# Attention stage: the 512-column products of TensorE that nobody reads are left out from the second batch on

## What is computed

```python
x = x + 0.5 * ffn(layernorm(x))          # 8 experts, top 2
x = x + attn(layernorm(x))
x = x + 0.5 * ffn(layernorm(x))

def attn(x):                              # B 8, S 256, E 128, H 16, HD 8
    q, k, v = (x @ w_q.T), (x @ w_k.T), (x @ w_v.T)      # as (B, S, H, HD)
    q, k = rope(q), rope(k)
    att = softmax(einsum('bqhd,bkhd->bhqk', q, k) / sqrt(HD))
    return einsum('bhqk,bkhd->bqhd', att, v).reshape(B, S, 128) @ w_o.T
```

## Time and profile before

| | us |
|---|---|
| median of 3 runs | 477.1 (476.74 to 477.88) |
| the profiled execution, its own time | 477.5 |
| its span, first to last instruction | 475.2 |
| TensorE busy | 400.3 |
| VectorE busy | 333.3 |
| ScalarE busy | 259.5 |
| GpSimd busy | 221.1 |

### The profile page before, as it was taken

How to read it: one execution, slowest core, us unless ns; L and a number is a source line. 1 busy time by engine, 2 the same in 40 slices (tenths; PEclk the granted TensorE clock), 3 DMA queues, 4 the chain that set the end, 5 groups by cost and what they waited for, 6 DMA issues and landing times.

```text
span 475.2 us, 10124 instructions
## 1 busy us (share of the span) xinstructions
PE 400.3 (84%) x3108; PEld 318.6 (67%) x3108; DVE 333.3 (70%) x1090; ACT 259.5 (55%) x525; POOL 221.1 (47%) x284
## 2 busy tenths in 40 slices
PE   4781885999899998989899999896889789999940
PEld 3551475989789875666766767673668679998830
DVE  4644762555877678778898988875537666558985
ACT  1332542766555646576675767573676256666610
POOL 4375653676553433133243542515035566645551
PEclk9786897999999997799999999999999799999975
DMA  9711531123211203992000000001111112133322
GB/s 269 285 53 37 173 117 50 40 63 86 65 51 41 74 24 117 331 320 59 2 23 13 12 14 13 24 8 35 35 39 47 51 50 62 57 109 95 107 63 70
DMA packets 33201, 37.78 MB, mean 80 GB/s; under 512 B 5504, under 2 KB 28032, under 8 KB 32752
## 3 DMA queue, kind: packets, MB, share of 16 engines
q1 hardware_dynamic: 28144, 27.36, 19.4%
q0 software_dynamic: 4544, 9.35, 5.9%
q10 hardware_dynamic: 464, 0.45, 0.5%
HBM read 26.71 MB, written 20.36 MB: 99 GB/s over the span
## 4 chain that ended last, share of the span: by engine, by line
PE 39%; DVE 10%; ACT 5%; issue 4%; another core or an unknown queue 2%; POOL 1%; POOLq 0%; DVEq 0%; ACTq 0%
PE ps L998 6%; PE ps L821 3%; PE ps L927 3%; PE ps L807 3%; PE ps L794 2%; PE ps L664 2%; DVE ring_lo L1882 2%; PE ps L882 2%; PE ps L822 2%; ACT stage L1356 2%; PE ps L1007 2%; PE ps L907 2%; PE ps L796 2%; PE ps L795 2%
## 5 line engine op out<-in xcount | busy, mean ns | idle before, releaser
L1882 DVE TENSOR_REDUCE ring_lo<-ps 128x4 fp32r<-128x1024 f32 x64 | 78.0, 1219 | 15.7 <-PE ps L916 15.6
L1300 ACT ACTIVATE stage<-ps 128x512 f32<-128x512 f32 x78 | 46.6, 597 | 76.9 <-PE ps L796 62.2
L1356 ACT ACTIVATE stage<-ps 128x1024 f32<-128x1024 f32 x64 | 65.4, 1022 | 21.2 <-PE ps L927 19.7
L821 PE MATMUL ps<-w_hl,ring_hi 128*128 x234 | 65.7, 349 | 7.4 <-issue 5.0
L1775 DVE TENSOR_TENSOR ring_hi<-ps,ring_hi 128x512 fp32r<-128x512 f32 x78 | 53.8, 690 | 16.4 <-ACT ring_hi L1307 12.0
L822 PE MATMUL ps<-w_hl,ring_hi 128*128 x312 | 61.4, 238 | 0.0
L537 POOL DMA_INDIRECT expert_y<-stage x39 | 38.3, 983 | 48.3 <-DVE stage L1783 45.4
L504 POOL DMA_INDIRECT sorted_x<-rows,place_at x32 | 31.9, 997 | 60.0 <-DVE place_at L1590 44.7
L537 POOL DMA_INDIRECT expert_y<-stage,arena x39 | 38.7, 993 | 40.7 <-DVE stage L1783 35.8
L1769 DVE TENSOR_TENSOR bx<-ps,bx 128x128 fp32r<-128x128 f32 x78 | 22.5, 289 | 50.1 <-ACT bx L1282 43.1
L822 PEld LDWEIGHTS ps<-w_hl,ring_hi 128*128 128x128 f32 x312 | 55.1, 195 | 0.0
(11 more groups left out here) (194 smaller groups left out, 963.2 us busy)
## 6 DMA issues: line engine op xcount, KB each, us to landing
sorted_x<-fill SPq DMA_DIRECT2D x8, 1096.5 KB, 16.7
stage<-w SPq DMA_DIRECT2D x16, 256.0 KB, 6.5
stage<-sorted_x SPq DMA_DIRECT2D x39, 64.5 KB
arena<-sorted_x SPq DMA_DIRECT2D x39, 64.5 KB
y_got<-expert_y SPq DMA_DIRECT2D x16, 128.0 KB, 2.3
stage<-expert_y SPq DMA_DIRECT2D x16, 128.0 KB, 2.4
x_tok<-x SPq DMA_DIRECT2D x4, 256.0 KB, 5.4
sorted_x<-rows,place_at POOLq DMA_INDIRECT x64
```

Of the source, the lines that this page charges most:

```text
L821: pe.matmul(both, bg_hi[:, s, c, :], w, start=(c == 0), stop=False, skip_group_check=True)
L1300: act.activation(g_full[:, s, :], ps[:, H_BANK, :], ACT.Gelu).then_inc(g_done, 1)
L1356: act.activation(prob[:, 2 * v:2 * v + 2, :], ps[:, at:at + 2, :], ACT.Exp, scale=SCALE)\
L1882: vec.tensor_reduce(shift_v[:, t, :, 24].rearrange("p (r g j) -> p r j g", r=2, g=2)[:, pair, 2 * jp:2 * jp + 2, :], ps[:, at:at + 2, :].r ...
```

## The change

All `keep_busy` products of the attention stage in batches 1 to 6 are left out, and the three at the start of batch 7: 21 + 12 + 6 + 10 = 49 products. With them go the waits that only they needed. Those of batch 0 stay, and so do the ten behind the start of batch 7. No other instruction is added, removed or moved, on any engine.

```diff
@@ step @@
-                if v == 0:
-                    pe.wait_ge(exp_done, STEPS * b + v + 1)
-                    keep_busy(EXP_BANK, 2 if b == 0 else 3)
+                if b == 0 and v == 0:
+                    pe.wait_ge(exp_done, 1)
+                    keep_busy(EXP_BANK, 2)
                 if scores_next:
                     scores_free(b + 1, v)
@@ batch, behind step 2 @@
                 if place_next:
                     if tail:
-                        scores_owned(b + 1, 3)
-                        keep_busy(2 * (3 % MAX_BUF), 2)
                         pe.wait_ge(y_ready, 2 * b - 1)
                     place(b + 1, q, 3, M1)
                 step(b, p, 3, place_next)
                 if place_next:
-                    if b:
-                        scores_owned(b + 1, 4)
-                        keep_busy(2 * (4 % MAX_BUF), 1)
-                    else:
+                    if b == 0:
                         pe.wait_ge(exp_done, STEPS * b + 4 + EXP_BUF)
                         keep_busy(EXP_BANK, 3)
                     pe.wait_ge(qk4_ready, 4 * b + 8)
@@ batch, behind step 4 @@
                     keep_busy(Y_BANK, 2)
                     router(FIRST_UNIT + b - 2)
                 elif b >= 2:
-                    scores_owned(b + 1, 5)
-                    keep_busy(2 * (5 % MAX_BUF), 2)
                     pe.wait_ge(yt_ready, b)
```

## The result

Medians of 20 executions each, on one chip: 473.47 us (468.76 to 479.75) against 475.87 us (474.26 to 480.58) of the kernel before. The ratio is 0.9953, interval 0.993 to 0.9976; ratios leave out the executions that took over 1.5% more than the fastest of the same kernel (here four of the 20, the profiled one among them), while medians and means are over all. The changed kernel is faster by 2.4 us, where the forecast was a time 2.8 us longer. The profiled execution took 477.69 us, and its span is 475.4 us; before it was 477.5 and 475.2. So the two profiles alone would show no difference, because this execution had the clock low for longer than most: the mean granted clock is 0.917 here and was 0.932 there.

What follows compares the result with a forecast made beforehand. The prediction took TensorE as the busiest engine, 400.3 of 475.2 us. From 477.5 us it took 3.4 for products on the path, added 6.2 for two clock falls (480.3), and forecast a median of 479.9 us, range 473.0 to 487.5.

Steps and rivals of the forecast that it cites:

- Start of the batch: Three products at the start of batches 1 to 7: 0 us in six batches, covered by ACT's copies; batch 7 taken as 0.
- The wait for "issue": PE's unexplained 2.03 us wait in batch 7, 5.5 us behind the scores, taken as what ends last there.
- Pair ahead of the fourth placing: Two products there in batches 1 to 6: 0.55 us gained in four batches, 0.48 in batches 4 and 5, 3.2 us.
- the single: One product ahead of the transposes in batches 1 to 6: 0 us, since the transposes wait for ACT's copy anyway.
- the router pair: Two products ahead of the router in batches 2 to 6: 0.3 us in batch 2, 0 later through DVE's queue.
- The price of low clock: From batch 0 against batch 1, steps 4 to 7: each us of low clock costs 0.32 us.
- The length of a fall and their sum: In the attention stage a fall lasts 6.5 to about 10 us and costs 3.1 us; two cost 6.2 us.
- The number of falls: Lean stretch from fourth placing to second projection, six batches: a fall in one batch in three, 2 falls; the weakest number.
- if a fall costs far from 3 us: Sign in the changed kernel's trace that the price from batch 0 doesn't carry over to the later batches.
- the clock holds everywhere: Rival: no fall in the attention stage, so the gain stands alone, 473.7 us or 472.8 with batch 7; chance 0.28.
- Falls in nearly every batch: Rival: 5 falls, at PE in steps 4 to 6 of each batch, 489.2 us; chance 0.10 for five or more.
- the gain is taken up: Rival: clock holds, but DVE or ACT's copies end last and the 0.55 us become PE idle time; 477.1 us, chance 0.07.

Runs made afterwards that it cites:

- e1: Only the three products at the start of batches 1 to 7 (21) left out of the kernel before; ratio 0.9993 to it.
- e8: e4 and e6 together, against the kernel before: 444.07 us, ratio 0.9904.
- e4: Kernel before without the pairs at fourth placing and router, with two products added ahead of the second projection in batches 1 to 5; ratio 0.9942.
- e12: e8 once more, on chip C, against the kernel before: 475.67 us, ratio 0.9906.
- e6: Only the three products at the start of batch 7 left out of the kernel before; ratio 0.9983.
- e3: Only the pair ahead of the fourth placing (12 products) left out of the kernel before; ratio 0.9938.
- e5: The changed kernel itself, unchanged, run once more on chip B against the kernel before; ratio 0.9948.
- e2: Kernel before with the products at the batch starts kept and the other 28 left out; ratio 0.9981.
- e7: Only the single product ahead of the transposes and the pair ahead of the router (16) left out of the kernel before; ratio 1.0046.
- e11: The changed kernel with the router pair of batch 6 alone put back, against the kernel before; ratio 0.995.
- e9: The changed kernel with two products put ahead of the second projection in batches 1 to 5, against the kernel before; ratio 0.9949.

## Why the forecast was wrong, step by step

**Start of the batch: right in batches 1 to 6, too low in batch 7.** 0 us in batches 1 to 6, with ACT's copies as the cover: the idle time of 1.08 us (changed) and 1.07 us (e1) that was asked for is there, and e1's ratio is 0.9993. In batch 7 I took 0 out of 0 to 0.89. e8 against e4 shows 0.85 us, so on chips A and B the upper end was right. The wait for "issue" on which the choice rested is PE waiting for ACT's copy of line 1361, which itself came late (3.27 us idle in the kernel before, 4.12 in e12). It goes with the occasion and not with the three products: before has them and e12 has not, and both show it; e4 has them and e6 has not, and in both PE's row of line 1007 has no wait ahead of it. Where ACT is late like that, it ends last and the three products may be free; that was not measured. What ACT waited for stays open, since the profile doesn't name it.

**Pair ahead of the fourth placing: right by name, near in size.** 3.2 us were worked out, and the single and the router pair at 0 and 0.3. The sum of these was 3.5 us, and e8 against e6 shows 3.0: 0.48, 0.47, 0.45, 0.44 and 0.50 us in batches 1 and 3 to 6, 0.63 in batch 2, where the router pair adds to it. (0.16 us, by e3, which keeps it; 0.3 was worked out.) The limit of 0.48 us from ACT's idle time, which I had set for batches 4 and 5 alone, held about everywhere. The middle batch without a fall takes 20.9 us, not the 20.5 to 20.7 that I named: the gain is right, but I took it off a mean (21.1 us) over batches that differ.

**The price of low clock: right inside the attention stage.** 0.32 us per us was worked out from batch 0 against batch 1. Over the 20 executions of the changed kernel, the least-squares line of time over low clock has a slope of 0.32 (standard error 0.05, correlation 0.84), with low clock from 64.7 to 86.4 us. But that agreement is partly luck: the same program gave 0.21 (0.06) in e5, and the kernel before 0.10, 0.07 and 0.22 on A, B and C. These slopes count low clock in the whole program, and not all of it costs: the profiled execution of e2 had 54.8 us of it, the most of its 12 executions, 27.3 of them ahead of 160 us, and it was the fastest of the 12. The single falls are the better measure: 0.7 us for 3.4 us (e2 batch 4, e5 batch 3, against 20.87), 1.0 us in batch 3 of the changed kernel (21.84), 1.25 in batch 6 of e5 (18.63 against the 17.38 of e8), that is 0.2 to 0.37 us for each.

**The length of a fall and their sum: this step failed.** I took "at least the 6.5 us of the row at 373.0 and at most about the 10 us of that at 185.2", 3.1 us per fall, 6.2 for two. In batches 3 to 6 of the changed kernel the three falls are 3.4 us long, and so are the two of e5 and the one of e2. Such a fall costs 0.7 to 1.25 us. My rows had no fall in this kind of work; both ends of the bound came from other places, and the lower one did not hold here. Longer ones do occur (6.8 us twice in e7 at some 2.4 us each, 10.2 us in batch 7 of the changed kernel in one profile and not in that of e5), so the length alone doesn't make the whole difference. Over all executions 2 x 6.5 to 2 x 10 us of low clock were forecast, 13 to 20 us more than before; the mean grew by 47.5 - 44.8 = 2.7 us (e5, uncertain by 3.4) and, with one pair kept, by 79.3 - 76.8 = 2.5 us (e11, uncertain by 3.6). Times 0.32 that is an estimate of 0.8 us where 6.2 were put down; read from e5's profile, its two falls cost 0.7 + 1.25 = 2.0 us. On the first chip the growth isn't known: the 20 executions of the changed kernel have a mean of 74.0 us, and of the kernel before only the profiled one has a clock on record, some 65 us.

**The number of falls.** "One batch in three", two in six: the changed kernel's profile has three in batches 3 to 6 and e5's has two. That count was fair for one profile. But low clock is a mean over executions, and that the kernel before has none of it in the attention stage past 195 us was read from one execution; whether its others have some can't be said, since only one was profiled.

With the measured sizes the sum is 3.0 + 0.85 - 0.8 = 3.0 us of gain, or 1.9 with the 2.0 us of e5's two falls. Measured are 2.4 us (changed, interval 1.1 to 3.3) and 0.9948 of 448.4, 2.3 us (e5). The forecast had -3.4 + 6.2 in their place. Its sign hung on the clock's term, and "if a fall costs far from 3 us" was named as the sign of it. That the time of 473.47 us lies inside the stated range is owed in part to the kernel before, which the range took at 477.1 and which 20 executions put at 475.87.

**The rivals.** That the clock holds everywhere (473.7 us) comes nearest by its number, but not by its mechanism, and so by luck: the clock fell three times in batches 3 to 6. The rule of the Trainium skill that stood behind it (TensorE: Matmul & The Clock Gate, section "Why this matters for your kernels"), that it is idle gaps that cool the clock, is not borne out here: ahead of the fall at 249.4 the longest idle time of PE in 3.4 us was 0.34 us, and in batch 7 the clock stood low for 10.1 us in which PE had work all the time. "Falls in nearly every batch" did not come, and "the gain is taken up" is refuted by e8 against e6.

**What stays open.** Which products keep the clock up is not settled. The lean stretch in front of the router is busy for 3.10 of 3.40 us in e4, where the clock held, and for 2.75 to 2.78 in the changed kernel and e7, where it fell in batches 3 and 6 and held in batch 4. The first pair of numbers is of different work, since e4 has the single product in it; the second is of the same work with either outcome, and that speaks for what I argued, that it depends on how the stretch lies against the moments at which the throttle decides. No run moved the stretch alone, so this is argued and not shown. Nor does the number of products left out order the low clock: against the kernel before on the same chip, 16 left out give 10.1 us more (e7), 28 give 8.2 (e2), all 49 give 2.7 (e5), 12 give 3.8 (e3), each uncertain by 2 to 5 us. Each run was profiled once, so the places of its falls are one draw out of many. And the plainest kernel was not run: only what costs left out, the pairs ahead of the fourth placing (e3) and the three of batch 7 (e6), with all else in its place. It would say whether e8 owes anything to its moved pairs.

## What to carry to other kernels

Before you price an event, such as a fall of the clock, look for one in the same kind of work; if the profile has none, let the bound reach to below the shortest one seen elsewhere: here the price per us of low clock carried over from another batch, and its amount was forecast some five times too large, and at least twice. A filler product costs nothing where its engine waits anyway and nearly its whole length (0.44 to 0.5 us a pair of 0.55) where it doesn't, so strike out only what costs and keep what is free: e8 has 34 fillers for the 49, ten of them in a wait, and is faster than the version without any, 0.9904 against 0.9948 on the same chip (1.9 us, uncertain by 1.4). The moved pair by itself is not shown to help (e9). And where a mechanism varies between executions, compare many of them: the two profiles here differ by 0.2 us and the medians by 2.4.

## What was not expected of the hardware

- The same program took 475.87, 447.96, 448.36 and 481.21 us on four occasions. Batches 1 to 5 are equal in length on all of them to within 0.3 us by the kernels profiled there (20.60 to 20.62, 21.00, 21.34 to 21.35 for the first three), so the difference of 7% lies elsewhere: the first exponential of the attention stage comes some 16 us earlier on A and B, the second expert phase with the end took 122 us there and 130 to 134 elsewhere, and batches 6 and 7 took some 4 us less. Where they are longer, ACT stood idle for up to 4.12 us for "remote" in batches 6 and 7; on A and B it never did there.
- Within one kernel on one chip the low clock ranged from 64.7 to 86.4 us, and the time followed it over 11 us.
- Lengths of low clock in the attention stage were 3.4, 6.8 and 10.2 us in all the profiles read.
- With PE busy for 2.75 to 2.78 of 3.40 us (changed kernel), the same stretch brought the clock down in one batch and not in the next.
